# Whole token tiles instead of single 128x128 blocks in the attention output transpose of an eight-core transformer layer kernel

## What is computed

```python
x = x + attn_a(layernorm(x))    # causal softmax attention, 16 heads of 64
x = x + ffn(layernorm(x))       # routing to 64 slots
x = x + attn_b(layernorm(x))    # a recurrence (wkv6) with projections
x = x + ffn(layernorm(x))
```

```python
def proj(w):
    y = jnp.einsum('bsh,oh->bso', hidden_states, w)
    return y.reshape(B, S, nh, hd).transpose(0, 2, 1, 3)
q, k, v = proj(Wq), proj(Wk), proj(Wv)
# by windows of 1024 queries, causal mask, softmax:
out = softmax(q @ k.T * scale + mask) @ v
out = out.transpose(0, 2, 1, 3).reshape(B, S, H)
return jnp.einsum('bsh,oh->bso', out, Wo)
```

## Time and profile before

| what | value |
|---|---|
| time, median of 2 runs | 6712.07 us (6710.11 and 6714.03) |
| the profiled execution's own time | 6717.25 us |
| its span, slowest core (core 3) | 6714.8 us |
| spans of the 8 cores | 6680.2 to 6714.8 us |
| PE, DVE, ACT busy on core 3 | 38%, 32%, 29% of the span |
| mean granted TensorE clock | 0.60 of 2.4 GHz |
| DMA | 45 GB/s over the span |

### The profile page before, as it was taken

How to read it: one execution, slowest core, us unless ns; L and a number is a source line. 1 busy time by engine, 2 the same in 40 slices (tenths; PEclk the granted TensorE clock), 3 DMA queues, 4 the chain that set the end, 5 groups by cost and what they waited for, 6 DMA issues and landing times.

```text
span 6714.8 us, 43273 instructions; the slowest of 8 cores (6680.2 to 6714.8 us)
## 1 busy us (share of the span) xinstructions
PE 2569.7 (38%) x13290; PEld 1162.2 (17%) x13290; DVE 2164.4 (32%) x4480; ACT 1960.2 (29%) x3022; POOL 142.3 (2%) x144
## 2 busy tenths in 40 slices
PE   2555555646223211333425243443435343232221
PEld 1222222222111100111112111121111211111110
DVE  1212212121122222353544545353544535122222
ACT  2454444546044200131221213122130313044300
POOL 0000000000000000000000000000000000000000
PEclk9656656565666655656656565655656565655655
DMA  4000000000411144400000000000000000411145
GB/s 76 13 25 26 26 26 26 15 36 1 83 37 38 38 100 174 66 0 25 0 25 0 20 6 0 25 1 25 0 25 0 1 25 0 82 38 38 33 83 186
DMA packets 87423, 242.87 MB, mean 36 GB/s; under 512 B 7837, under 2 KB 17181, under 8 KB 87072
## 3 DMA queue, kind: packets, MB, share of 16 engines
q0 software_dynamic: 59936, 135.04, 8.6%
q1 hardware_dynamic: 27264, 105.06, 4.8%
HBM read 235.03 MB, written 67.11 MB: 45 GB/s over the span
## 4 chain that ended last, share of the span: by engine, by line
PE 31%; DVE 24%; ACT 23%; DMA 11%; issue 7%; another core or an unknown queue 1%; POOL 1%; DVEq 1%; ACTq 0%; POOLq 0%; PEld 0%; PEldq 0%; SPq 0%
PE psC L1759 4%; ACT Wslot L594 4%; ACT L594 4%; DVE b_ubuf L1709 3%; ACT hfeat L333 2%; ACT hfeat L328 2%; DVE b_mixb L1717 2%; PE psC L665 2%; PE psC L2223 2%; PE psC L1785 2%; ACT hfeat L399 2%; PE psT L388 2%; DMA x2d<-xout 2%; PE psC L580 1%; DMA xin<-x 1%
## 5 line engine op out<-in xcount | busy, mean ns | idle before, releaser
L388 PE MATMUL psT<-identb_s,htok 128*128 128x128 bf16 x832 | 96.9, 309 | 902.4 <-DVEq L369 812.5
L328 ACT ACT_TABLE_LOAD x34 | 43.6, 1283 | 1151.4 <-DMA xin<-x2d 498.0
L594 ACT ACT_TABLE_LOAD x192 | 246.3, 1283 | 273.9 <-PE psC L580 273.9
L1949 PE MATMUL psT<-identb_s,b_xx 128*128 128x128 bf16 x256 | 32.4, 306 | 735.1 <-DVE b_xx L1937 735.1
L1759 PE MATMUL psC<-b_mixb,Wslot 128*128 128x512 bf16 x1024 | 256.9, 418 | 44.7 <-DVE b_mixb L1717 44.7
L608 DVE TENSOR_TENSOR Wslot<-Wslot,maskA_s 128x512 bf16<-128x512 bf16 x128 | 54.4, 425 | 613.5 <-ACT Wslot L594 613.5
L1815 ACT ACT_TABLE_LOAD x8 | 10.3, 1283 | 809.7 <-PE psD L1806 809.7
L388 PEld LDWEIGHTS psT<-identb_s,htok 128*128 128x128 bf16 x832 | 84.6, 142 | 919.4 <-issue 919.4
L580 PE MATMUL psA<-Qf,Kf 64*128 64x512 bf16 x192 | 108.4, 565 | 265.0 <-ACT Wslot L594 257.5
L340 DVE TENSOR_SCALAR stats<-stats 128x4 f32<-128x4 f32 x34 | 5.8, 170 | 595.1 <-ACT hfeat L333 595.1
L594 ACT ACTIVATE Wslot<-psC,cvals_s 128x256 bf16<-128x256 f32 (+2 forms) x384 | 175.0, 515 | 0.0
(11 more groups left out here) (378 smaller groups left out, 6092.9 us busy)
## 6 DMA issues: line engine op xcount, KB each, us to landing
xin<-x1d SPq DMA_DIRECT2D x32, 2048.0 KB, 10.0
x1d<-xout POOLq DMA_DIRECT2D x16, 2048.0 KB, 13.6
xin<-x SPq DMA_DIRECT2D x10, 2048.0 KB, 11.0
x2d<-xout POOLq DMA_DIRECT2D x8, 2048.0 KB, 13.6
xin<-x2d SPq DMA_DIRECT2D x8, 2048.0 KB, 11.4
out<-xout POOLq DMA_DIRECT2D x8, 2048.0 KB, 13.4
Wslot<-fWhhT POOLq DMA_DIRECT2D x6, 2048.0 KB, 16.1
Wslot<-fWihT POOLq DMA_DIRECT2D x6, 2048.0 KB, 16.3
```

The source lines that it names most:

```text
L328: ctx.inc(sc.activation(scr[:, tt * 1024:(tt + 1) * 1024], xin[:, tt, :], AF.Square, accum_out=stats[:, 8 + tt:9 + tt]), "AC")
L388: ctx.inc(t.transpose(psT[:, bank + dc * 128:bank + (dc + 1) * 128], hb[:, tt, dc * 128:(dc + 1) * 128], identb[:]), "PE")
L594: ctx.inc(sc.activation(Ph[:, kt * 512 + qo:(kt + 1) * 512], ps[:, 0:512 - qo], AF.Exp, bias=cvals[:, 1:2], scale=0.125), "AC")
```

## The change

For each of the 4 token tiles of a block, PE now makes all 8 transposes in one step, into the 8 pieces of one whole bank of `psT`, and DVE copies the bank to `Ofeat` with one instruction of 1024 columns (8 runs of 128, written 512 columns apart). The banks alternate by token tile. The wait is now one per token tile: the transposes of `tt` wait for the copy of `tt - 2`; the first two have no such wait. The number of transposes, the data, `psT` and `Ofeat` are unchanged; 256 copies become 32. Everything behind this stretch moves up by one line number in the changed file.

```diff
-            pingT = Ping(2)
-            i = 0
+            prev_te = [None, None]
             for tt in range(BT):
-                for dc in range(NDC):
-                    half = i % 2
-
-                    def f_tp(t, tt=tt, dc=dc, half=half):
-                        if tt == 0 and dc == 0:
-                            ctx.wait(t, "DV")
-                        pingT.acquire(lambda s, v: t.wait_ge(ctx.sem[s], v), half)
-                        ctx.inc(t.transpose(psT[:, half * 1024:half * 1024 + 128],
-                                            Otok[:, tt, dc * 128:(dc + 1) * 128],
-                                            identb[:]), "PE")
-                    ctx.on("tensor", f_tp)
-                    pe_v = ctx.c["PE"]
-
-                    def f_te(v, tt=tt, dc=dc, half=half, pe_v=pe_v):
-                        ctx.wait(v, "PE", pe_v)
-                        ctx.inc(v.tensor_copy(Ofeat[:, dc, tt * 128:(tt + 1) * 128],
-                                              psT[:, half * 1024:half * 1024 + 128]),
-                                "DV")
-                    ctx.on("vector", f_te)
-                    pingT.release(half, "DV", ctx.c["DV"])
-                    i += 1
+                bank = (tt % 2) * 1024
+
+                def f_tp(t, tt=tt, bank=bank, pte=prev_te[tt % 2]):
+                    if tt == 0:
+                        ctx.wait(t, "DV")
+                    if pte is not None:
+                        t.wait_ge(ctx.sem["DV"], pte)
+                    for dc in range(NDC):
+                        ctx.inc(t.transpose(
+                            psT[:, bank + dc * 128:bank + (dc + 1) * 128],
+                            Otok[:, tt, dc * 128:(dc + 1) * 128],
+                            identb[:]), "PE")
+                ctx.on("tensor", f_tp)
+                pe_v = ctx.c["PE"]
+
+                def f_te(v, tt=tt, bank=bank, pe_v=pe_v):
+                    ctx.wait(v, "PE", pe_v)
+                    ctx.inc(v.tensor_copy(
+                        Ofeat[:, :, tt * 128:(tt + 1) * 128],
+                        psT[:, bank:bank + 1024].rearrange(
+                            "p (a b) -> p a b", b=128)), "DV")
+                ctx.on("vector", f_te)
+                prev_te[tt % 2] = ctx.c["DV"]
```

## The result

The changed kernel took 6667.41 us (median of 11 runs, 6647.79 to 6683.87) beside 6715.17 for the kernel before (10 runs, 6697.36 to 6731.65): a ratio of 0.9926, 95% interval 0.9911 to 0.9942. So the gain is about 50 us in one and 75 us (70 by its ratio) in the other, with the forecast of 59 between them.

A forecast was written before the change was run, and what follows sets the result against it. The PE-DVE round trip bounds the stretch, no engine being near full: 96.7 - 8 x 4.75 = 58.7 us off 6717.25 gives 6658.5, or 6653 us against the median; 8-in-10 range 6632 to 6670 us.

The forecast's parts named there:

- The stretch is wholly on the chain: Attention, first transpose to first output-projection matmul: nothing covers it, eight blocks total 96.7 us, 1.4% of the span.
- The schedule on paper: New stretch of one block: copies end at 1.82, 2.63, 3.79 and 4.60 us, projection starts at 4.75 us.
- The copy, 0.69 us: DVE's 1024-column copy out of PSUM: 0.69 us, carried on from shorter rows; bounds 0.43 and 1.225 us.
- Rival A: New copy moves one element per cycle, 1.225 us each: 12 us more in all, 6665 us; chance 0.08.
- The removed branches cost nothing: Removed branches and waits in the stretch: no cost of their own, already inside the 0.74 us of a round.
- Rival B: Dense transposes raise PE's clock before the output projection: 19 us more gain, 6634 us; chance 0.13.
- the first 16 matmuls stay at 5.96 us: Output projection, first token tile: the clock still rises only within its matmuls, so 5.96 us, not 3.61.
- Everything behind only moves up: Load, next block and later sublayers start earlier by what the stretch loses; other sublayers unchanged in length.
- The 8 us that I kept on either side for the clock's shift: Clock rises in later stretches fall a little earlier or later: 1 us per block either way, sign open.

The follow-up runs named there:

- steps8: Changed kernel with each of a group's 8 transposes in a step of its own, waits on the first; ratio 0.9904 (0.9882 to 0.9927).
- filled: Changed kernel plus 18 unread matmuls per block, 10 ahead of the first transposes and 8 behind the last; ratio 0.9897 (0.9877 to 0.9917).

## Why the prediction was right, and where it was not

- *The stretch is wholly on the chain*: right. Its 59.4 us are found again in attention, which lost 69.9 us, the sum of the stretch's 59.4 and the projection's 10.6.
- *The schedule on paper*: right within 0.03 us at each step. The transposes came from rows in which the same operation stood without a wait, the copy was carried on from shorter ones.
- *The copy, 0.69 us*: right, 692 ns as a median, 3-dimensional output and gaps included. Rival A falls. VectorE: DVE Perf Modes in the Trainium skill, section "Why PSUM operands drop a tier", caps what an operand in PSUM allows, and the trace agrees at 1024 columns too: (692 - 224) / 896 = 0.52 ns per column, the pace of the shorter copies.
- *The removed branches cost nothing*: right on PE (`steps8`), not tested on DVE.
- *Rival B, at 0.13, against "the first 16 matmuls stay at 5.96 us"*: this step failed. B came true in 35 to 39 of 64 blocks, 4.6 a core, and gave 10.6 us, close to B's own price of 2.35 us a block (10.9). My argument was that the layer norm's runs of 16 transposes stand at 0.50. I take it that this compared the wrong things: behind those 16 PE waits 3.46 us for ACT, while the new stretch has 32 with short gaps. That more work on PE there brings the rise forward in every block is shown by `filled`; why 25 to 29 blocks stayed late without it is open. TensorE: Matmul & The Clock Gate in the Trainium skill, section "PE-mode transpose", says that the full clock does not engage for transposes; the windows of the fifth block show the clock rising within them, so the measurement decides against it.
- *Everything behind only moves up*: this failed by 10 us, in a sublayer that I had not looked at. In the sum the two misses cancel: 59.4 + 10.6 - 10.0 = 60 us against 58.7 forecast. The right total is partly luck, and the measured median of the first series, 6667.41 us, lies 14 us above the 6653 us forecast. The 8 us that I kept on either side for the clock's shift were of about the right size for each.

## What to carry to other kernels

Two engines that pass small pieces to and fro pay the hand-over, not the work: count the hand-overs on the chain, and give each as much as the buffer holds. Here 6.2 of the 7.3 us that the stretch lost came with the fewer waits, and 1.1 with the larger instruction. Where TensorE has to be idle ahead of a dense stretch, look at the granted clock in the first matmuls, and in all that follow: matmuls whose result is thrown away raised it in time, but it then fell earlier too, in a pause of 2.21 us across which it had held with a later rise. And compare the sublayers that were not touched as well, as means over the cores.

## What the hardware did that I had not expected

- VectorE stands still for 0.46 us at fixed places of its instruction list, 128 rows of the trace or a multiple of that apart, with a packet of 8192 bytes close behind. An edit that removes instructions or waits moves all later pauses to other instructions.
- In the routing blocks of the last sublayer the clock rose, once the cores had settled, either about 2.8 or about 5.9 us after the first matmul (2.4 or 5.5 on some cores), and the late case made a block 3.2 us longer (61.55 against 58.32). A block that started 0.4 us later could fall into the late case, so 0.4 us cost 3.
- Sixteen VectorE copies of 128 columns in a row take 0.14 us each (2.19 us in all), though the profile gives one 0.21 to 0.225 us.
